# A graph kernel on one core: a DRAM copy in parts of 80 rows, key and digit rows in four buffers each, adding scatters of two groups outstanding

## The chip, the cores and the metric

The kernel runs on one core of a Trainium2 chip. The metric is the device time of one execution in microseconds. The kernel before has a median of 1702.86 us in 3 runs (1702.32 to 1704.51).

## What is computed

There are 50,000 nodes with 256 features each (x), 12,500 edges from `src` to `dst`, with `dst` sorted, and 128 features for every edge. Two layers, cut to what matters:

```
# layer 0, attention over the edges that end in a node
h   = x @ Wn.T + bn
a   = leaky_relu(sum((h[src] + edge_attr @ We.T + be) * attn))
a   = softmax of a over the edges with the same dst
x1  = layernorm(x + relu(segment_sum(h[src] * a, dst)))
# layer 1, mean of neighbours; here the edges are summed by src
agg = segment_sum(x1[dst], src)
out = layernorm(x1 + x1 @ W1.T + b1 + (agg / count) @ W2.T + b2)
```

Most nodes have no edge. So the sum z = x + relu(...) is x for most rows, with a few thousand rows changed.

## The kernel before

Edges are handled in T = 100 tiles of 128, in Q = 25 groups of GT = 4 tiles. The work runs in stages, in the same order on all engines:

1. **Set-up and edge features** (to 80 us). SyncE loads edge features into the four buffers `xin` (lines 349 to 361), twelve loads of eight tiles and two of one; a load waits until VectorE has used the buffer (`s_eau`). VectorE makes a dot product for every tile (`feature_dot`, L783).
2. **Two counting sorts**, by `dst` and then by `src` (80 to 470 us). For each sort VectorE and ScalarE make one-hot rows of all keys' digits (`onehots`, `high_onehots`), TensorE adds them to a histogram, and then, group by group, TensorE adds a tile's one-hots to a table (`count_tile`, L1173), ScalarE copies the table (L648), TensorE looks the tile's keys up in it (L1222), and VectorE reads the found ranks (`found_rank`, `ranks`, `tiles`, L842). Each group needs its keys and its low digits spread over all 128 partitions: SyncE loads both from DRAM (L370, L372), each into two buffers (`lowB`, `kB`), and waits for `s_lbT`, `s_lbA` and `s_kbu` before it overwrites one. ScalarE's part of the digits (`upper_across`, L616) stands one group ahead, in the middle of its table copies (L649).
3. **GpSimd beside them.** It scatters each tile's edges to their sorted places with an indirect transfer (`scatter_order`, L469, at most FLIGHT = 6 outstanding), loads the order, and from the seventh group of the second sort on it gathers the rows x[src] into `X` (L485 to 488). Then it scatters the first 20 tiles of the second sort (`order_src(20)`, L499).
4. **Softmax weights** (to 515 us), from dots of the gathered rows, on VectorE.
5. **First aggregation** (515 to 868 us), `by_dst` on all engines: per group TensorE sums weighted rows with matrices that VectorE makes from the sorted keys (`select`, L987; keys loaded by `load3`, L380), multiplies by Wn, ScalarE cuts at zero into `xin` (L674), and GpSimd adds the four tiles to `z_scratch` with four adding indirect scatters (L508). Rows that aren't the last of their node go to spare rows behind row N. GpSimd waits before a group until the scatters of the group before have landed (L505, L506). Until the first of them `z_scratch` must hold all of x (L500).
6. **Dense stage** (868 to 1455 us) over all 50,000 rows of z, 98 groups, and **second aggregation** (to the end).

**The copy of x to z_scratch** runs from DRAM to DRAM in NCOPY = 100 parts on SyncE's queue (`copy_x`, L344). A part takes every hundredth block of 4 rows of x, which is 125 rows of 4 KB, 500 KB in all. The parts are placed by hand in SyncE's order: 8 before the fifth load of features, one behind each of the first sort's 25 groups, 24 behind the second group of the second sort (two whenever two more groups of one-hots are ready), 11 beside the later groups, and the remaining 32 once the first two loads of sorted keys are issued (L391). The loads of sorted keys of the third group and on come behind those (L392).

Of the kernel before, what the change touches and what calls it, by code (L numbers as in the profile page):

```python
# [5 lines left out]
P = 128  # L6
# [46 lines left out]
def build(nc, x, src, dst, edge_attr, Wn, bn, We, be, attn, W1, b1, W2, b2, out):  # L53
# [14 lines left out]
    NEC = FT // EC  # L68
    NCOPY = 100
    assert N % (NCOPY * GT) == 0  # L70

    z_dram = nc.dram_tensor("z_scratch", [N + 6 * P, D], F32).ap()
    keyrow_dram = [nc.dram_tensor(f"keys_scratch{k}", [T, P], F32).ap() for k in (DST, SRC)]
# [4 lines left out]
    with ExitStack() as ctx:  # L78
        def sb(name, shape, dt=F32):
            return ctx.enter_context(nc.sbuf_tensor(name, shape, dt))  # L80
# [4 lines left out]
        def sems(name, n):  # L85
            return [sem(f"{name}{i}") for i in range(n)]
# [77 lines left out]
        zeros = sel[0]  # L164
        trash_i = sb("trash_i", [P, T], I32)
        trash = sb("trash", [P, T])
# [8 lines left out]
        aggn = sb("aggn", [P, GT, D])  # L175
        lowB = [aggn[:, i, :].bitcast(BF16) for i in range(2)]
        spare16 = aggn[:, 2:4, :].rearrange("p j c -> p (j c)").bitcast(BF16)
# [34 lines left out]
        s_seed = sem("table_seeded")  # L212
        s_kb = sems("key_spread", 2)
        s_kbu = sem("key_spread_used")
        s_lb = sems("low_digit_spread", 2)
        s_lbT = sem("low_onehot_across_ready")
# [104 lines left out]
        def full(ap):  # L321
            return ap[:].rearrange("p j d -> p (j d)")
# [5 lines left out]
        def _(sp):  # L328
# [12 lines left out]
            def part_of(table):  # L341
                return table.rearrange("(r c k) d -> c r (k d)", c=NCOPY, k=GT)

            def copy_x(n):  # L344
                for c in range(copied[0], min(copied[0] + n, NCOPY)):
                    sp.dma_start(part_of(z_dram[0:N])[c], part_of(x)[c]).then_inc(s_copy, 16)  # L346
                copied[0] = min(copied[0] + n, NCOPY)

            for c in range(NEC):
                if c == 4:  # L350
                    copy_x(8)
                wait(sp, s_eau, EC * (c - 3))
                v = edge_attr[0:NEC * EC * P].rearrange("(c t p) d -> p c t d", p=P, t=EC)
                sp.dma_start(full(xin[c % 4]).rearrange("p (t d) -> p t d", d=DE),
                             v[:, c:c + 1].rearrange("p a t d -> p (a t) d")).then_inc(s_ea[c % 4], 16)
# [8 lines left out]
            for k in (DST, SRC):  # L364
                sp.wait_ge(s_keyd[k], 32)
                for q in range(Q):
                    n = k * Q + q
                    wait(sp, s_lbT, n - 1)
                    wait(sp, s_lbA, n - 1)
                    sp.dma_start(lowB[n % 2], spread(lowrow_dram[k], q)).then_inc(s_lb[n % 2], 16)  # L370
                    wait(sp, s_kbu, n - 1)
                    sp.dma_start(full(kB[n % 2]), spread(keyrow_dram[k], q)).then_inc(s_kb[n % 2], 16)  # L372
                    if k == DST or q >= 2 and q % 2:
                        copy_x(1)
                    if k == SRC and q == 1:
                        for i in range(Q // 2):
                            sp.wait_ge(s_onehot, Q + 2 * i + 1)
                            copy_x(2)

# [40 lines left out]
        def _(pool):  # L420
# [5 lines left out]
            g.iota(iota_i, pattern=[[1, LO]], base=0, channel_multiplier=0)  # L426
            g.iota(trash_i[:], pattern=[[0, Q], [P, GT]], base=N + 1, channel_multiplier=1).then_inc(s_iota, 1)
            g.memset(ones[:], 1.0)
# [71 lines left out]
            pool.wait_ge(s_copy, 16 * NCOPY)  # L500
            pool.wait_ge(s_zero, 48)

            for q in range(Q):
                pool.wait_ge(s_relu, 2 * q + 2)
                if q:  # L505
                    pool.wait_ge(s_zsc[(q - 1) % 4], 16 * GT * ((q - 1) // 4 + 1))  # L506
                for j in range(GT):
                    g.indirect_dma_start(out=z_dram, out_offset=column(idx_out[DST], GT * q + j), in_=xin[q % 4][:, j, :],  # L508
                                         in_offset=None, compute_op=ALU.add).then_inc(s_zsc[q % 4], 16)
# [36 lines left out]
        def _(act):  # L546
# [29 lines left out]
            act.wait_ge(s_const, 2)  # L576
            for i in range(3):
                act.dma_start(z_dram[N + 2 * i * P:N + 2 * (i + 1) * P].rearrange("(p r) d -> p (r d)", r=2),
                              full(zeros)).then_inc(s_zero, 16)
# [36 lines left out]
            def upper_across(k, q):  # L616
                n = k * Q + q
                act.wait_ge(s_lb[n % 2], 16 * (n // 2 + 1))
                wait(act, s_look[k], GT * (q - 1))
                if k == SRC and q < 2:  # L620
                    act.wait_ge(s_look[DST], T)
                wait(act, s_lbA, n)
                made = gap(gap_low, lowB[n % 2], -1.0, slot_f[:, 1:2])
                is_zero(onehotT[n % 2][:, 1, :], gap_low, made).then_inc(s_lbA, 1)
# [9 lines left out]
            for k in (DST, SRC):  # L634
                if k == SRC:
                    act.wait_ge(s_add[DST], T)
                for q in range(Q):
                    high_onehots(k, q)
                act.wait_ge(s_hotA, (k + 1) * Q)
                if k == DST:  # L640
                    act.wait_ge(s_bias, 1)
                    act.wait_ge(s_zero, 48)
                upper_across(k, 0)
                act.wait_ge(s_seed, k + 1)
                for i in range(T // 2):
                    wait(act, s_add[k], 2 * i)
                    wait(act, s_look[k], 2 * (i - 1))
                    a.copy(table[i % 2].rearrange("p b c -> p (b c)"), bank[2][:, 0:2 * HC]).then_inc(s_tab, 1)  # L648
                    if i % 2 == 0 and i // 2 + 1 < Q:  # L649
                        upper_across(k, i // 2 + 1)  # L650
                    if k == SRC and i == 2 * ORDER_AT + 5:
                        store_sorted(DST)
# [81 lines left out]
        def _(dve):  # L734
# [19 lines left out]
            v.tensor_copy(iota16[:], iota_i)  # L754
            v.tensor_copy(trash[:], trash_i[:])

# [65 lines left out]
            def low_across(k, q):  # L822

                n = k * Q + q
                dve.wait_ge(s_lb[n % 2], 16 * (n // 2 + 1))
                wait(dve, s_look[k], GT * (q - 1))
                if k == SRC and q < 2:
                    dve.wait_ge(s_look[DST], T)
                ts(onehotT[n % 2][:, 0, :], lowB[n % 2], slot_f[:, 0:1], None, ALU.is_equal).then_inc(s_lbT, 1)

# [11 lines left out]
            def tiles(k, between):  # L842
                low_across(k, 0)
                for q in range(Q):
                    n = k * Q + q
                    for f in between.get(q, ()):
                        f()
                    dve.wait_ge(s_kb[n % 2], 16 * (n // 2 + 1))
                    keys = full(kB[n % 2])
                    for j in range(GT):  # L850
# [541 lines left out]
```

## Time and profile before

| | us |
|---|---|
| median of 3 runs | 1702.86 |
| profiled execution, its own time | 1711.68 |
| its span | 1709.9 |
| TensorE busy | 1276.8 (75%) |
| VectorE busy | 1089.1 (64%) |
| ScalarE busy | 782.5 (46%) |
| GpSimd busy | 747.8 (44%) |
| bytes moved | 260.18 MB, mean 152 GB/s |

All times in the rows are microseconds from the start of the span unless marked otherwise. PE is TensorE, DVE is VectorE, ACT is ScalarE, POOL is GpSimd, and SPq is the queue of SyncE, whose entries are issues of transfers, not the transfers themselves. A bracket behind an instruction gives the idle time of its engine before it and what ended it. The share of a DMA queue is the time that its packets took, as a share of 16 engines' time in the stretch.

### The profile page before, as it was taken

How to read it: one execution, taken by the hardware profiler on the slowest of the kernel's cores; microseconds unless marked ns; L12 is line 12 of the kernel's file. 1: busy time of each engine (PE TensorE's matmuls, PEld its weight loads, DVE VectorE, ACT ScalarE, POOL GpSimd, SP SyncE). 2: the span in 40 equal slices, each digit the busy share in tenths (PEclk: the TensorE clock that was granted, in tenths of full speed). 3: DMA queues.
4: the chain of work that ended last, by engine and by line, in shares of the span. 5: the costliest groups of instructions: out<-in, count | busy, mean ns of one | idle time of the engine just before them, and what ended most of it. 6: DMA issues, size and time to landing. Idle time of an engine off the chain costs nothing.

```text
span 1709.9 us, 26717 instructions
## 1 busy us (share of the span) xinstructions
PE 1276.8 (75%) x7210; PEld 1075.5 (63%) x7210; DVE 1089.1 (64%) x3970; ACT 782.5 (46%) x1768; POOL 747.8 (44%) x731
## 2 busy tenths in 40 slices
PE   4367672276703079988259999999999899999995
PEld 3266652165602068876148888888888688877784
DVE  8655581165691045543048888889898878777762
ACT  6333381143301034443127777777777545444442
POOL 1056630046771046566634443025553336555553
PEclk9689996599856589999669999999999999999998
DMA  4655533367643345555456666678998423232221
GB/s 142 193 147 159 159 118 132 133 168 197 197 168 130 140 88 81 80 80 59 53 136 220 221 220 218 226 238 292 303 296 284 158 70 97 85 91 89 90 85 44
DMA packets 118873, 260.18 MB, mean 152 GB/s; under 512 B 21973, under 2 KB 55340, under 8 KB 118796
## 3 DMA queue, kind: packets, MB, share of 16 engines
q1 hardware_dynamic: 76738, 193.81, 34.5%
q0 software_dynamic: 40128, 64.45, 17.7%
q10 hardware_dynamic: 1930, 1.06, 0.2%
q8 instruction: 28, 0.46, 0.1%
q14 instruction: 49, 0.40, 0.1%
HBM read 182.23 MB, written 129.96 MB: 183 GB/s over the span
## 4 chain that ended last, share of the span: by engine, by line
PE 40%; DMA 22%; SPq 12%; POOL 10%; DVE 8%; issue 6%; ACT 1%; POOLq 0%; ACTq 0%; DVEq 0%
PE bank L1244 25%; DMA aggn<-low_digits_scratch 12%; SPq L346 11%; PE bank L1234 7%; POOL z_scratch L508 5%; DMA z_scratch<-xin,idx_out 5%; DVE X L745 3%; DMA xin<-z_scratch,idx_src 3%; PE bank L1241 3%; POOL out_rows L463 3%; POOL xin L460 2%; PE bank L1289 2%; PE bank L1285 2%; DMA xin<-in_edge_attr 1%; DMA kB<-sorted_scratch 1%
## 5 line engine op out<-in xcount | busy, mean ns | idle before, releaser
L1244 PE MATMUL bank<-w1T,xT 128*128 128x256 f32 x1968 | 492.1, 381 | 0.0
L1244 PEld LDWEIGHTS bank<-w1T,xT 128*128 128x128 f32 x1968 | 344.0, 191 | 66.5 <-issue 0.3
L469 POOL DMA_INDIRECT order_scratch<-pay,rank_i x200 | 194.6, 973 | 257.6 <-DVE rank_i L840 108.1
L562 ACT ACTIVATE yout<-bank,nmr,rstd 128x256 f32<-128x256 f32 x492 | 251.1, 576 | 9.0 <-DVE nmr L748 9.0
L508 POOL DMA_INDIRECT z_scratch<-xin,idx_out x100 | 156.5, 1565 | 188.8 <-DMA z_scratch<-in_x 85.3
L913 DVE BATCH_NORM_STATS2 stats<-xin 128x6 f32<-128x512 f32 x246 | 158.2, 685 | 114.2 <-DMA xin<-z_scratch,idx_src 57.4
L1173 PE MATMUL bank<-X 128*128 128x196 bf16 x800 | 101.6, 265 | 164.0 <-ACT sel L648 140.3
L553 ACT COPY xT<-bank 128x512 f32<-128x512 f32 x346 | 202.9, 588 | 39.9 <-PE bank L1234 32.2
L661 ACT COPY agg<-bank 128x257 f32<-128x257 f32 (+1 forms) x200 | 74.2, 371 | 300.0 <-PE bank L1289 293.6
L913 DVE BATCH_NORM_STATS2 stats<-bank 128x6 f32<-128x512 f32 x246 | 168.4, 693 | 60.3 <-PE bank L1244 59.8
L1173 PEld LDWEIGHTS bank<-X 128*128 128x128 bf16 x800 | 70.5, 104 | 195.3 <-ACT sel L648 155.9
L1285 PE MATMUL bank<-X,sel 128*128 (+2 forms) x400 | 124.6, 395 | 80.6 <-DVE csel L745 80.6
L1222 PE MATMUL bank<-sel,agg 128*128 128x196 f32 x800 | 174.8, 368 | 0.0
L745 DVE TENSOR_SCALAR xin<-xin,stats,rstd 128x256 f32<-128x256 f32 x492 | 172.7, 413 | 1.0
L1234 PE MATMUL bank<-ident,xin 128*128 128x128 f32 x984 | 132.4, 274 | 50.6 <-DVE xin L745 50.6
L557 ACT ACTIVATE std<-stats,eps_c 128x4 f32<-128x4 f32 x271 | 80.9, 299 | 184.9 <-DVE stats L913 176.2
L1241 PE MATMUL bank<-bias,ones 128*128 128x256 bf16 (+1 forms) x592 | 162.1, 274 | 3.2 <-ACT xT L553 2.7
L460 POOL DMA_INDIRECT X<-in_x,idx_src x100 | 98.7, 987 | 150.0 <-DVE idx_out L899 115.1
L463 POOL DMA_INDIRECT out_rows<-yout,idx_out x100 | 99.9, 999 | 144.8 <-DMA xin<-z_scratch,idx_src 74.8
L1234 PEld LDWEIGHTS bank<-ident,xin 128*128 128x128 f32 x984 | 117.7, 142 | 66.0 <-issue 51.2
L460 POOL DMA_INDIRECT X<-z_scratch,idx_dst x100 | 94.8, 948 | 140.8 <-DVE xin L745 110.1
L1222 PEld LDWEIGHTS bank<-sel,agg 128*128 128x128 f32 x800 | 151.5, 217 | 0.2
(187 smaller groups left out, 1915.4 us busy)
## 6 DMA issues: line engine op xcount, KB each, us to landing
z_scratch<-in_x SPq DMA_DIRECT2D x100, 500.0 KB
xin<-z_scratch SPq DMA_DIRECT2D x97, 512.0 KB, 4.1
out_rows<-yout SPq DMA_DIRECT2D x97, 512.0 KB, 3.1
kB<-keys_scratch SPq DMA_DIRECT2D x50, 256.0 KB, 4.7
kB<-sorted_scratch SPq DMA_DIRECT2D x50, 256.0 KB, 3.5
aggn<-low_digits_scratch SPq DMA_DIRECT2D x50, 128.0 KB, 8.6
xin<-in_edge_attr SPq DMA_DIRECT2D x12, 512.0 KB, 6.6
order_scratch<-pay,rank_i POOLq DMA_INDIRECT x200, 5.2
```

What stands on the lines that cost most here:

```text
L346: sp.dma_start(part_of(z_dram[0:N])[c], part_of(x)[c]).then_inc(s_copy, 16)
L460: g.indirect_dma_start(out=dst_ap, out_offset=None, in_=table, in_offset=where).then_inc(s, 16)
L469: g.indirect_dma_start(out=order_dram[k], out_offset=bass.IndirectOffsetOnAxis(ap=rank_i[k][:, t:t + 1], axis=0), in_=pay[:, t, :], in_off ...
L508: g.indirect_dma_start(out=z_dram, out_offset=column(idx_out[DST], GT * q + j), in_=xin[q % 4][:, j, :], in_offset=None, compute_op=ALU.ad ...
L553: a.copy(xT[dst_i][:].rearrange("p a b c -> p (a b c)"), src_bank[:, :]).then_inc(copied, 1)
L562: a.activation(yout[hu][0:rows, j, :], bank_of(j // 2)[0:rows, (j % 2) * D:(j % 2 + 1) * D], ACT.Identity, bias=nmr[0:rows, slot, j:j + 1] ...
L745: return v.tensor_scalar(o, i, s1, s2, o0, o1) if o1 is not None else v.tensor_scalar(o, i, s1, s2, o0)
L913: return v.bn_stats(stats[0:rows, slot, 2 * p:2 * p + 2, :].rearrange("p j s -> p (j s)"), pair.rearrange("p j c -> p c j"))
L1222: ins = mm(bank[3 + t % 4][:, 0:HC], onehotT[n % 2][:, b, j * P:(j + 1) * P], table[i % 2][:, b, :], start=b == 0, stop=b == 1)
L1234: ins = tr(o[:, at:at + n], buf[0:n, 2 * p + jj, c * P:(c + 1) * P], ident[0:n, 0:n])
L1241: mm(to, ones16[:, 0:n], bias16[:, bias, :], start=True, stop=False)
L1244: ins = mm(to, buf[:, jj, c, 0:n], w[:, c, :], start=False, stop=i == len(terms) - 1 and c == 1)
```

## The change

- The copy has 125 parts instead of 100. A part takes every 125th block of 5 rows: 80 rows of 5 KB, 400 KB in all. 12 parts go before the fifth load of features; none stands beside the lookups of either sort; 36 go behind the fourth group of the second sort (three whenever two more groups of one-hots are ready); the remaining 77 go where the last 32 went.
- The spread keys and low digits have four buffers each. They lie in `yout`, which is free until the dense stage; `kB` keeps the sorted keys alone.
- GpSimd waits for the scatters of the group before the last one, so two groups' scatters may be outstanding. The spare rows behind row N are therefore eight blocks in turn instead of four (`trash_i`), and five instead of three transfers clear them. `trash_i` moves into a buffer that is free at that time.

```diff
-    NCOPY = 100
-    assert N % (NCOPY * GT) == 0
-
-    z_dram = nc.dram_tensor("z_scratch", [N + 6 * P, D], F32).ap()
+    NCOPY, CR = 125, 5
+    assert N % (NCOPY * CR * 16) == 0
+
+    z_dram = nc.dram_tensor("z_scratch", [N + 10 * P, D], F32).ap()
...
-        trash_i = sb("trash_i", [P, T], I32)
+        TS = -(-T // (2 * GT)) * 2 * GT
+        trash_i = xT[2][:].rearrange("p a b c -> p (a b c)").bitcast(I32)[:, 0:TS]
...
-        lowB = [aggn[:, i, :].bitcast(BF16) for i in range(2)]
+        lowB = [yout[i][:, 2, :].bitcast(BF16) for i in range(4)]
+        keyB = [yout[i][:, 0:2, :].rearrange("p j c -> p (j c)") for i in range(4)]
...
-                return table.rearrange("(r c k) d -> c r (k d)", c=NCOPY, k=GT)
+                return table.rearrange("(r c k) d -> c r (k d)", c=NCOPY, k=CR)
...
-                    copy_x(8)
+                    copy_x(12)
...
-                    wait(sp, s_lbT, n - 1)
-                    wait(sp, s_lbA, n - 1)
-                    sp.dma_start(lowB[n % 2], spread(lowrow_dram[k], q)).then_inc(s_lb[n % 2], 16)
-                    wait(sp, s_kbu, n - 1)
-                    sp.dma_start(full(kB[n % 2]), spread(keyrow_dram[k], q)).then_inc(s_kb[n % 2], 16)
-                    if k == DST or q >= 2 and q % 2:
-                        copy_x(1)
-                    if k == SRC and q == 1:
+                    wait(sp, s_lbT, n - 3)
+                    wait(sp, s_lbA, n - 3)
+                    sp.dma_start(lowB[n % 4], spread(lowrow_dram[k], q)).then_inc(s_lb[n % 4], 16)
+                    wait(sp, s_kbu, n - 3)
+                    sp.dma_start(keyB[n % 4], spread(keyrow_dram[k], q)).then_inc(s_kb[n % 4], 16)
+                    if k == SRC and q == 3:
                         for i in range(Q // 2):
                             sp.wait_ge(s_onehot, Q + 2 * i + 1)
-                            copy_x(2)
+                            copy_x(3)
...
-            g.iota(trash_i[:], pattern=[[0, Q], [P, GT]], base=N + 1, channel_multiplier=1).then_inc(s_iota, 1)
+            g.iota(trash_i, pattern=[[0, TS // (2 * GT)], [P, 2 * GT]], base=N + 1, channel_multiplier=1).then_inc(s_iota, 1)
...
-                if q:
-                    pool.wait_ge(s_zsc[(q - 1) % 4], 16 * GT * ((q - 1) // 4 + 1))
+                if q >= 2:
+                    pool.wait_ge(s_zsc[(q - 2) % 4], 16 * GT * ((q - 2) // 4 + 1))
...
-            for i in range(3):
+            for i in range(5):
                 act.dma_start(z_dram[N + 2 * i * P:N + 2 * (i + 1) * P].rearrange("(p r) d -> p (r d)", r=2),
                               full(zeros)).then_inc(s_zero, 16)
```

ScalarE and VectorE take the digits and keys from buffer n % 4 instead of n % 2.

## Rows read from the trace of the kernel before

**Rows 1.** The page's section 4, the chain that ended last, its shares by line

```profile
PE bank L1244 25%; DMA aggn<-low_digits_scratch 12%; SPq L346 11%; PE bank L1234 7%; POOL z_scratch L508 5%; DMA z_scratch<-xin,idx_out 5%; DVE X L745 3%; DMA xin<-z_scratch,idx_src 3%; PE bank L1241 3%; POOL out_rows L463 3%; POOL xin L460
```

**Rows 2.** DMA view of 540 to 580 us; queue line: packets, MB, share of 16 engines

```profile
DMA packets 1337, 5.26 MB, mean 132 GB/s; under 512 B 52, under 2 KB 52, under 8 KB 1337
...
q1 hardware_dynamic: 1337, 5.26, 32.0%
```

**Rows 3.** DMA views of the dense stage, 1000 to 1100 and 1200 to 1300 us

```profile
DMA packets 7008, 22.22 MB, mean 222 GB/s; under 512 B 1589, under 2 KB 1603, under 8 KB 7008
...
DMA packets 8861, 29.74 MB, mean 297 GB/s; under 512 B 1605, under 2 KB 1605, under 8 KB 8859
```

**Rows 4.** Timeline of SyncE's queue: start us, us, line, out<-in, count

```profile
22.95 19.53 SPq L346 DMA_DIRECT2D z_scratch<-in_x  x8
...
89.74 0.74 SPq L346 DMA_DIRECT2D z_scratch<-in_x  x1
...
227.39 85.15 SPq L346 DMA_DIRECT2D z_scratch<-in_x  x24
```

**Rows 5.** Timeline of VectorE, the first feature dot behind the copies; idle before in brackets

```profile
62.07 0.29 DVE L748 SCALAR_TENSOR_TENSOR xin<-xin,u_b 128x128 f32<-128x128 f32 x1 [11.30 <-DMA xin<-in_edge_attr]
```

**Rows 6.** Timeline of TensorE, lookups of both sorts; idle before in brackets

```profile
82.15 0.83 PE L1173 MATMUL bank<-X 128*128 128x196 bf16 x4 [0.58 <-ACT sel L648]
...
91.09 0.50 PE L1173 MATMUL bank<-X 128*128 128x196 bf16 x4
...
225.30 0.33 PE L1169 MATMUL bank<-zero 128*128 128x392 bf16 x1
...
265.19 0.83 PE L1173 MATMUL bank<-X 128*128 128x196 bf16 x4 [0.58 <-ACT sel L648]
...
331.65 0.84 PE L1173 MATMUL bank<-X 128*128 128x196 bf16 x4 [58.90 <-ACT sel L648]
...
334.87 0.50 PE L1173 MATMUL bank<-X 128*128 128x196 bf16 x4
...
338.73 0.50 PE L1173 MATMUL bank<-X 128*128 128x196 bf16 x4
```

**Rows 7.** Timelines of VectorE and TensorE, from the last row dot on

```profile
502.79 0.08 DVE L748 DVE_READ_ACCUMULATOR xT<-X,v_b 128x1 f32 x1
...
530.35 1.03 PE L1244 MATMUL bank<-wnT,xT 128*128 128x256 f32 x4
608.61 1.23 PE L1285 MATMUL bank<-X,sel 128*128 128x257 f32 x2 [77.23 <-DVE csel L745]
```

**Rows 8.** Timeline of GpSimd, adding scatters; last line from the chain of waits

```profile
606.03 1.63 POOL L508 DMA_INDIRECT z_scratch<-xin,idx_out  x1 [85.29 <-DMA z_scratch<-in_x]
...
621.00 1.58 POOL L508 DMA_INDIRECT z_scratch<-xin,idx_out  x1 [7.68 <-ACT xin L674]
...
704.10 1.56 POOL L508 DMA_INDIRECT z_scratch<-xin,idx_out  x1 [2.95 <-DMA z_scratch<-xin,idx_out]
...
714.19 1.56 POOL L508 DMA_INDIRECT z_scratch<-xin,idx_out  x1 [2.93 <-DMA z_scratch<-xin,idx_out]
...
864.48 3.79 DMA z_scratch<-xin,idx_out
```

**Rows 9.** Timeline of TensorE, first aggregation, the same step of two neighbouring groups

```profile
703.69 0.60 PE L1285 MATMUL bank<-X,sel 128*128 x2
...
711.93 0.60 PE L1285 MATMUL bank<-X,sel 128*128 x2
```

**Rows 10.** Timeline of GpSimd, order scatters (first line: the page's group: count, busy, mean ns) and gathers

```profile
L469 POOL DMA_INDIRECT order_scratch<-pay,rank_i x200 | 194.6, 973 | 257.6 <-DVE rank_i L840 108.1
...
245.37 0.64 POOL L480 DMA_DIRECT2D ordrow<-order_scratch  x1 [9.15 <-DMA order_scratch<-pay,rank_i]
...
361.11 1.02 POOL L460 DMA_INDIRECT X<-in_x,idx_src  x1 [115.10 <-DVE idx_out L899]
...
493.62 1.08 POOL L460 DMA_INDIRECT X<-in_x,idx_src  x1 [0.30 <-issue]
```

More of the change, by code:

```diff
@@ L212, in build @@
         s_seed = sem("table_seeded")
-        s_kb = sems("key_spread", 2)
+        s_kb = sems("key_spread", 4)
         s_kbu = sem("key_spread_used")
-        s_lb = sems("low_digit_spread", 2)
+        s_lb = sems("low_digit_spread", 4)
         s_lbT = sem("low_onehot_across_ready")
@@ L500, in _ @@
             pool.wait_ge(s_copy, 16 * NCOPY)
-            pool.wait_ge(s_zero, 48)
+            pool.wait_ge(s_zero, 80)
             for q in range(Q):
                 pool.wait_ge(s_relu, 2 * q + 2)
-                if q:
-                    pool.wait_ge(s_zsc[(q - 1) % 4], 16 * GT * ((q - 1) // 4 + 1))
+                if q >= 2:
+                    pool.wait_ge(s_zsc[(q - 2) % 4], 16 * GT * ((q - 2) // 4 + 1))
                 for j in range(GT):
@@ L617, in upper_across @@
                 n = k * Q + q
-                act.wait_ge(s_lb[n % 2], 16 * (n // 2 + 1))
+                act.wait_ge(s_lb[n % 4], 16 * (n // 4 + 1))
                 wait(act, s_look[k], GT * (q - 1))
@@ L622, in upper_across @@
                 wait(act, s_lbA, n)
-                made = gap(gap_low, lowB[n % 2], -1.0, slot_f[:, 1:2])
+                made = gap(gap_low, lowB[n % 4], -1.0, slot_f[:, 1:2])
                 is_zero(onehotT[n % 2][:, 1, :], gap_low, made).then_inc(s_lbA, 1)
@@ L641, in _ @@
                     act.wait_ge(s_bias, 1)
-                    act.wait_ge(s_zero, 48)
+                    act.wait_ge(s_zero, 80)
                 upper_across(k, 0)
@@ L754, in _ @@
             v.tensor_copy(iota16[:], iota_i)
-            v.tensor_copy(trash[:], trash_i[:])
+            v.tensor_copy(trash[:], trash_i[:, 0:T])
             def key_rows(k):
@@ L824, in low_across @@
                 n = k * Q + q
-                dve.wait_ge(s_lb[n % 2], 16 * (n // 2 + 1))
+                dve.wait_ge(s_lb[n % 4], 16 * (n // 4 + 1))
                 wait(dve, s_look[k], GT * (q - 1))
@@ L828, in low_across @@
                     dve.wait_ge(s_look[DST], T)
-                ts(onehotT[n % 2][:, 0, :], lowB[n % 2], slot_f[:, 0:1], None, ALU.is_equal).then_inc(s_lbT, 1)
+                ts(onehotT[n % 2][:, 0, :], lowB[n % 4], slot_f[:, 0:1], None, ALU.is_equal).then_inc(s_lbT, 1)
             def found_rank(k, t):
@@ L847, in tiles @@
                         f()
-                    dve.wait_ge(s_kb[n % 2], 16 * (n // 2 + 1))
-                    keys = full(kB[n % 2])
+                    dve.wait_ge(s_kb[n % 4], 16 * (n // 4 + 1))
+                    keys = keyB[n % 4]
                     for j in range(GT):
```

## The prediction

> **What bounds the kernel now.** I read the chain that ended last first. TensorE's dense products have 25% of it, and the change doesn't touch them. The load of the low digits has 12%, the issue of the copy of x (SPq L346) 11%, the adding scatters and their landings 5% and 5% [rows 1]. These are the stages before 868.3 us, where the last adding scatter lands; all after it, 1709.9 - 868.3 = 841.6 us, I leave as it is. The profiled execution took 1711.68 us with a span of 1709.9; the median of the runs, 1702.86, is 8.8 us lower. I take my difference off the median.
>
> Second, the copy by itself, where nothing else runs: 132 GB/s, with 32.0% of the time of 16 DMA engines used [rows 2]. 32% is 5 of 16 (31%), and a part has 125 rows = 5 x 25: I read it as five engines at 26.3 GB/s each, eleven idle. Loads and stores of 128 rows don't look so: the dense stage moves 222 and 297 GB/s [rows 3].
>
> Third, the stages. The eight early copies keep SyncE's queue from 22.95 to 42.5 us [rows 4], and VectorE then waits 11.30 us for edge features behind them [rows 5]. The first sort's lookups take 82.15 to 225.30 us, 143.15 for 25 groups. In the second sort the burst of 24 copies holds SyncE for 85.15 us [rows 4], the digits of the third group can't be issued until it is over, and TensorE stands for 58.90 us [rows 6]. At the end TensorE stands 77.23 us for sorted keys that are queued behind the copy [rows 7], and the adding scatters wait 85.29 us for it, to 606.03; the last lands at 864.48 + 3.79 = 868.3 [rows 8]. Last, GpSimd runs one group of adding scatters in 714.19 - 704.10 = 10.09 us, of which 2.95 is the wait for the group before to land [rows 8]; TensorE's own group is 711.93 - 703.69 = 8.24 us [rows 9].
>
> **The copy's parts.** 80 rows = 16 x 5, so all 16 engines should share one: 80 x 5,120 bytes = 0.41 MB each; 12 parts go early (4.9 MB), 36 in the burst (14.75 MB), 77 at the end (31.5 MB). The rate is the large unknown. Bounds: below, 132 GB/s (no gain); above, 16 x 26.3 = 420. The nearest row with 16 engines at work on 4 KB rows is the 297 of the dense stage [rows 3], which wasn't yet short of transfers, so I take somewhat more, **330 GB/s**, and keep 297 and 420 for the range. Issuing is no limit: 0.74 us a part [rows 4] is 57 us for 77. The Trainium skill ("DMA: Bandwidth & Descriptors", section on why a DMA increments its semaphore by 16) says that a transfer runs on the largest number of engines up to 16 that divides its slowest dimension on both sides: 5 for 125 rows and 16 for 80. The 32.0% agrees.
>
> **Features.** 4.9 MB is over at 23 + 15 = 38 us, before the fifth load of features is issued. Of the 11.30 us I take back 9.3 (0 to 11.3; a load still has to land). First lookup 82.15 - 9.3 = 72.9.
>
> **First lookups.** Where digits and keys are there, a group takes 338.73 - 334.87 = 3.86 us [rows 6]. With four buffers and no copy beside them, I let all groups run so; the first two took 91.09 - 82.15 = 8.94 instead of 7.72 us, 1.2 more. 25 x 3.86 + 1.2 = 97.7, a gain of 45.4 (bounds: 0, were the loads late anyway, and 45.4). End at 170.6. GpSimd's order scatters do not keep up: 0.97 us and 0.3 between two are 5.1 a group, so they end near 207, wait some 9 us as before [rows 10] and their load lands near 222. That is wanted only in the sixth group of the second sort, near 231: hidden, with 9 us to spare.
>
> **Second lookups.** One-hots and histogram keep their 265.19 - 225.30 = 39.9 us: first lookup at 210.5. ScalarE makes the digits of group q+1 in the middle of group q, and four groups are now loaded ahead of the burst, so the load behind it is wanted at 210.5 + 1.2 + 3 x 3.86 = 223.3, 50.6 us after the burst begins (227.39 - 54.7 = 172.7). At 330 GB/s the burst takes 44.7: no stall (from 291 GB/s down it is one). The 58.90 us go. Lookups end at 210.5 + 97.7 + 2 for the order columns = 310.
>
> **Gathers and softmax.** The 100 gathers took 1.34 us each (361.11 to 495.0, [rows 10]) and start with group 7, now 241: 375, landed 381. From the last dot to the first cut h it is 531.4 - 502.8 = 28.6 us [rows 7]: first scatter possible at 410. The gathers are what is late next: they outlast them by 65 us, and the 20 order scatters behind them on GpSimd (25 us) end at 400, hidden under the softmax.
>
> **The copy's end.** SyncE issues the 77 parts from 310 on. With 48 gathers left (6.3 MB) 37.8 MB go through: 115 us at 330, so 425. The copy is still last, by 15 us. The sorted keys of the third group come behind it, as now.
>
> **Adding scatters.** With two groups outstanding GpSimd needs 4 x (1.56 + 0.30) = 7.5 us a group, less than TensorE's 8.24, which becomes the pace. From the first scatter: 15.0 to the second group (621.00 - 606.03), 23 x 8.24 = 189.5, the last four 7.5, landing 3.8: 215.8 us, against 868.3 - 606.0 = 262.3, a gain of 46.5. TensorE's pace excludes more; below, no row shows two groups in flight, and rival 2 prices no gain. The two more clearing transfers, issued in the first 10 us on ScalarE's queue, cost nothing: their first reader is the lookups' table at 70 us; without that cover they would be some 1 us. The larger iota of spare indices likewise.
>
> **Sum.** 425 + 216 = 640.4 against 868.3: -228 us. 1702.9 - 228 = **1475**.
>
> **Rivals.**
> 1. *All 16 engines, but slower.* Every byte of the copy is both read from and written to DRAM, and no row shows 16 engines doing only that. At the 222 GB/s of the dense stage's first part [rows 3] the burst takes 66 us, a stall of 16, lookups end at 326, the copy at 496: 712, **1546**. The Trainium skill (same page, "Latency and other measured facts") gives 214 GB/s per direction as the full rate of copies between memory tensors; by it 1553. Nothing in this trace bears on it, since five engines reach 132. Chance 0.2.
> 2. *The scatters' pace stays 10.1 us* since two groups in flight only land later: 425 + 262 = 687, **1522**. For it: landings, not issue, are waited for. Against: 4 us of landing overlap 7.5 us of issue. Chance 0.1.
> 3. *Gathers suffer*: the copy used five engines and now uses all. At 2.0 us for each of the last 48, first scatter at 442: **1485**. Against: beside five busy engines they went at 1.38 us [rows 10]. Chance 0.1.
> 4. *Slower: the parts don't spread*, and the copy stays at 131 GB/s. Then taking 25 parts away from the lookups is a loss: features +6 us, burst 113 us with a stall of 62, lookups end at 388, the last 38 MB at 676: 892, +24, **1726**. It decides from about 138 GB/s down. Against: 5 of 16 fits 125 rows too well. This is also how the change would fail to do what it says. Chance 0.04.
>
> **Numbers.** The forecast's own case (297 to 420 GB/s) has 0.56 and reaches from 1454 (copy hidden under the softmax: 410 + 24 x 8.24 + 11.3 = 619) to 1488. Gathers at 1.26 us would take 8 more off: 1446. The range goes from 1446 to 1548, which takes in rivals 1 to 3. 0.2% (3.4 us; the runs lie 2.2 apart) is about what can be told from no change. Faster 0.95, same 0.01, slower 0.04.
>
> **What would show it.** Right: over 300 GB/s and a busy share near 0.9 in the tail of the copy, lookup groups of 3.9 us in both sorts, no stall after the burst, first adding scatter at 410 to 440, then 8.2 us a group. Wrong: a share of 0.32 in the tail (rival 4), a rate near 220 with all engines busy (1), scatters at 10 us (2), gathers at 2 us (3), or lookup groups over 5 us: then something other than digits paces them.

## The result, and the profile after

The changed kernel takes **1483.2 us** in the median of 4 runs (1479.6 to 1485.8), the kernel before 1703.3: a ratio of 0.8706 with a 95% interval of 0.8682 to 0.8730, or 220 us less. The forecast was 1475 (228 less). On another chip the same two gave 1483.2 and 1705.3. One execution of all, of the kernel e4_two_buffers below, took 3416.6 us instead of 1492; no trace of it was kept, its cause is open, and no figure here uses it.

The page of the profiled execution (its own time 1480.68 us): span, busy time, the 40 slices, and the chain that ended last.

```profile
span 1478.9 us, 26741 instructions
...
PE 1243.5 (84%) x7210; PEld 1049.3 (71%) x7210; DVE 1091.8 (74%) x3970; ACT 783.8 (53%) x1768; POOL 749.0 (51%) x731
...
DMA  6754695779975666656666766888974223332221
...
PE bank L1244 31%; PE bank L1234 8%; SPq L348 7%; PE bank L1222 5%; POOL out_rows L463 4%; DMA xin<-z_scratch,idx_src 4%; PE bank L1241 4%; POOL xin L460 4%; PE bank L1289 3%; PE bank L1285 3%; ACT aggn L600 3%; DVE X L745 2%; PE bank L1173 2%; DMA yout<-low_digits_scratch 2%; ACT sel L648 1%
```

The low digits' load had 12% of the chain [rows 1] and has 2%; the adding scatters and their landings, 5% and 5% before, are no longer listed. The issue of the copy is still there, with 7% instead of 11% (its line is now L348): the copy still sets when the adding scatters may begin.

SyncE's queue, the three places of the copy and the load behind the burst (start us, us, line, count):

```profile
24.11 8.69 SPq L348 DMA_DIRECT2D z_scratch<-in_x  x12
...
169.75 34.04 SPq L348 DMA_DIRECT2D z_scratch<-in_x  x36
205.79 0.33 SPq L372 DMA_DIRECT2D yout<-low_digits_scratch  x1
...
314.96 99.67 SPq L348 DMA_DIRECT2D z_scratch<-in_x  x77
```

Against [rows 4]: 24 parts held the queue for 85.15 us, 36 parts with a fifth more bytes in all (14.7 against 12.3 MB) hold it for 34.04.

TensorE, at the ends of its stages (start us, us, line; idle before in brackets):

```profile
70.74 0.83 PE L1173 MATMUL bank<-X 128*128 128x196 bf16 x4 [0.58 <-ACT sel L648]
...
167.69 0.33 PE L1169 MATMUL bank<-zero 128*128 128x392 bf16 x1
...
206.92 0.83 PE L1173 MATMUL bank<-X 128*128 128x196 bf16 x4 [0.58 <-ACT sel L648]
...
231.10 0.83 PE L1173 MATMUL bank<-X 128*128 128x196 bf16 x4 [9.55 <-ACT sel L648]
...
315.37 0.33 PE L1169 MATMUL bank<-zero 128*128 128x392 bf16 x1
385.96 0.46 PE L1264 MATMUL bank<-ident,xdot 128*100 128x128 f32 x1 [70.27 <-DVE xT L748]
...
413.06 1.03 PE L1244 MATMUL bank<-wnT,xT 128*128 128x256 f32 x4
435.76 1.23 PE L1285 MATMUL bank<-X,sel 128*128 128x257 f32 x2 [21.68 <-DVE csel L745]
```

Against [rows 6] and [rows 7]: the first sort's lookups take 97.0 us instead of 143.2, which is 25 groups of 3.86 and a slow start. The stall behind the burst is 9.55 us instead of 58.90, the wait for the keys behind the copy 21.68 instead of 77.23. The wait for the dots of the gathered rows is 70.27 us long; it was half of that before:

```profile
502.93 0.45 PE L1264 MATMUL bank<-ident,xdot 128*100 128x128 f32 x1 [35.19 <-DVE xT L748]
```

The lookups end earlier and the gathers keep GpSimd's own pace, so the last one is issued 64 us after the lookups' end (379.14 against 315.37), and its dots come 70 us after it.

GpSimd's first adding scatters (start us, us, line; idle before in brackets):

```profile
433.18 1.63 POOL L508 DMA_INDIRECT z_scratch<-xin,idx_out  x1 [24.79 <-DMA z_scratch<-in_x]
...
446.79 1.58 POOL L508 DMA_INDIRECT z_scratch<-xin,idx_out  x1 [6.31 <-ACT xin L674]
...
455.03 1.56 POOL L508 DMA_INDIRECT z_scratch<-xin,idx_out  x1 [1.07 <-ACT xin L674]
...
463.28 1.56 POOL L508 DMA_INDIRECT z_scratch<-xin,idx_out  x1 [1.09 <-ACT xin L674]
```

And from the chain of waits, the last one's landing:

```profile
641.36 3.72 DMA z_scratch<-xin,idx_out
```

Against [rows 8]: 463.28 - 455.03 = 8.25 us a group instead of 10.09, and what ends the wait is ScalarE's cut of h at zero, not a landing.

The copy nearly alone, DMA view of 409 to 417 us (a queue's line: packets, MB, time of its packets as a share of 16 engines):

```profile
DMA packets 719, 2.64 MB, mean 330 GB/s; under 512 B 206, under 2 KB 206, under 8 KB 718
...
q1 hardware_dynamic: 615, 2.62, 100.7%
```

The same view of 330 to 380 us, with the gathers beside the copy:

```profile
DMA packets 5005, 18.61 MB, mean 372 GB/s; under 512 B 1134, under 2 KB 1134, under 8 KB 5004
...
q1 hardware_dynamic: 3219, 13.74, 73.0%
```

And the busy shares of 414 to 434 us in 40 slices, in which the last parts land, with GB/s below them:

```profile
DMA  9999999999998999998999876432210000000000
GB/s 338 328 389 420 348 338 317 348 348 379 358 338 287 352 358 328 328 348 320 352 305 289 274 283 180 180 133 102 92 66 31 20 31 20 31 31 20 25 25 16
```

Against [rows 2]: 330 GB/s with all 16 engines busy, instead of 132 with 32.0%. That is 20.6 GB/s an engine against 26.3. The rate isn't even: 404 to 416 us gives 314 GB/s with 224 packets of the order scatters beside the copy, 416 to 424 us 341 with none. In the last rows the share begins to fall near 425 us, and from 429.5 to 433.2 us some 25 GB/s are left, with 6.2% of the 16 engines' time, which is one engine. The engines don't finish together, and the copy is done only when the last one is.

### The profile page after: what moved, and what is told of

It reads as the page before. It is cut to its first block, busy times and chain, and to the rows that moved or that the text cites. A ratio compares the mean times of both kernels' runs of the same rounds, so it can differ in the third digit from the quotient of the medians.

```text
span 1478.9 us, 26741 instructions
## 1 busy us (share of the span) xinstructions
PE 1243.5 (84%) x7210; PEld 1049.3 (71%) x7210; DVE 1091.8 (74%) x3970; ACT 783.8 (53%) x1768; POOL 749.0 (51%) x731
## 4 chain that ended last, share of the span: by engine, by line
PE 55%; POOL 9%; DMA 8%; issue 7%; ACT 7%; SPq 7%; DVE 6%; ACTq 0%; POOLq 0%; DVEq 0%
PE bank L1244 31%; PE bank L1234 8%; SPq L348 7%; PE bank L1222 5%; POOL out_rows L463 4%; DMA xin<-z_scratch,idx_src 4%; PE bank L1241 4%; POOL xin L460 4%; PE bank L1289 3%; PE bank L1285 3%; ACT aggn L600 3%; DVE X L745 2%; PE bank L1173 2%; DMA yout<-low_digits_scratch 2%; ACT sel L648 1%
## 5 line engine op out<-in xcount | busy, mean ns | idle before, releaser
L1222 PE MATMUL bank<-sel,agg 128*128 128x196 f32 x800 | 155.6, 338 | 0.1
L1173 PE MATMUL bank<-X 128*128 128x196 bf16 x800 | 94.4, 252 | 48.8 <-ACT sel L648 23.6
L1289 PE MATMUL bank<-agg,csel 128*128 128x257 f32 (+1 forms) x396 | 123.1, 393 | 12.2 <-ACT agg L661 12.2
L1222 PEld LDWEIGHTS bank<-sel,agg 128*128 128x128 f32 x800 | 133.0, 194 | 0.5 <-DVE bank L748 0.3
```

Of the source, the lines that this page charges most:

```text
L1222: ins = mm(bank[3 + t % 4][:, 0:HC], onehotT[n % 2][:, b, j * P:(j + 1) * P], table[i % 2][:, b, :], start=b == 0, stop=b == 1)
L1289: ins = mm(o, csel[u % 2][:, j, :], before, start=False, stop=True)
```

## Experiments

Where the expectation names the kernel before or the changed kernel, the difference is against these two. Between chips the medians of the kernel before were 1703.3 to 1705.6.

**How many engines carry a part.** The changed kernel, the same bytes in the same places, but parts of 125 rows (e2_rows125, the diff) and of 100 rows (e3_rows100, with `NCOPY, CR = 100, 5`).

```diff
-    NCOPY, CR = 125, 5
-    assert N % (NCOPY * CR * 16) == 0
+    NCOPY, CR = 100, 4
+    assert N % (NCOPY * CR) == 0
...
-                    copy_x(12)
+                    copy_x(10)
...
-                            copy_x(3)
+                            copy_x(3 if i < 5 else 2)
```

> The changed kernel, but with the copy in 100 parts of 125 rows of 4 KB as before (10 parts early, 29 in the burst, 61 at the end: the same bytes in the same places). Theory: the number of rows sets how many engines carry a part, 5 for 125, so the copy runs alone at 131 GB/s with a busy share near 0.32. Then the features start some 19 us later, the burst of 14.85 MB takes 113 us and the lookups stand for 60 to 70 us behind it, the end of the copy is near 640, and the time is 1690 to 1730 us, about that of the kernel before. Rival: bytes per row or the missing copies beside the lookups made the copy fast, not its row count; then it runs at over 250 GB/s here too and the time stays within 1475 to 1510.

Measured: **1713.2 us**, ratio 1.0036 [1.0009, 1.0064], so slower than before by 0.1 to 0.6%. The copy alone, 500 to 540 us:

```profile
DMA packets 1337, 5.27 MB, mean 132 GB/s; under 512 B 51, under 2 KB 51, under 8 KB 1337
...
q1 hardware_dynamic: 1337, 5.27, 32.0%
```

The same 132 GB/s and 32.0% as before. The last 61 parts end at 659 us, and what the other parts of the change give is lost again. That is the fourth rival, nearly at its price (1726). Not all of it is the five engines: e10_buffers_five_engines below has them too, but its parts in their old places, and takes 1611.1 us.

> The changed kernel, but with the copy in 100 parts of 100 rows of 5 KB (10 early, 29 in the burst, 61 at the end, the same bytes in the same places). With 80 rows all engines are busy, but each moves only 19.6 GB/s where the copy is alone, against 26.3 with five. Theory: that is a limit that all share, not the engines' own; 100 rows run on ten engines, a share of 0.62, at 25 to 26 GB/s each, 240 to 263 together, and the end of the copy is 5 to 20 us later: 1485 to 1505 us. Rival: rows of 5 KB cost each engine more, and ten give 196 GB/s; then the last 31 MB take some 175 us and the time is 1530 to 1560. Second rival: the row count doesn't matter in this way and all 16 engines stay busy: 1483.

Measured: **1517.6 us**, ratio 0.8883 [0.8824, 0.8942]. The copy alone, 430 to 448 us:

```profile
DMA packets 1022, 4.76 MB, mean 265 GB/s; under 512 B 92, under 2 KB 92, under 8 KB 1022
...
q1 hardware_dynamic: 1022, 4.76, 63.6%
```

63.6% is ten engines of 16 (62.5%), at 26.2 GB/s each with rows of 5 KB. So the row's size doesn't slow an engine: with the same rows of 5 KB ten engines give 26.2 each and sixteen 20.6, which points to something that they share. Both rivals fall. The time is 12 us above the theory's range all the same, and the copy's end came 34 us late (467.4 against 433.2), not 5 to 20. 10 us of this are there before the last parts start, mostly since the stall behind the burst is 18.46 us instead of 9.55. Then the copy is slower, by most beside the gathers, with 198 GB/s (340 to 370 us) where sixteen engines gave it 275:

```profile
q1 hardware_dynamic: 1274, 5.93, 48.1%
```

I had not counted that a part of the gathers' rows passes through the copy's ten engines and takes time there (48.1% instead of 63.6%).

**The buffers.** The changed kernel with two buffers each.

```diff
-                    wait(sp, s_lbT, n - 3)
-                    wait(sp, s_lbA, n - 3)
-                    sp.dma_start(lowB[n % 4], spread(lowrow_dram[k], q)).then_inc(s_lb[n % 4], 16)
-                    wait(sp, s_kbu, n - 3)
-                    sp.dma_start(keyB[n % 4], spread(keyrow_dram[k], q)).then_inc(s_kb[n % 4], 16)
-                    if k == SRC and q == 3:
+                    wait(sp, s_lbT, n - 1)
+                    wait(sp, s_lbA, n - 1)
+                    sp.dma_start(lowB[n % 2], spread(lowrow_dram[k], q)).then_inc(s_lb[n % 2], 16)
+                    wait(sp, s_kbu, n - 1)
+                    sp.dma_start(keyB[n % 2], spread(keyrow_dram[k], q)).then_inc(s_kb[n % 2], 16)
+                    if k == SRC and q == 1:
```

ScalarE and VectorE take the digits and keys from buffer n % 2 again.

> The changed kernel with two buffers each for keys and low digits, as before, and the burst behind the second group of the second sort, since only two groups can be loaded ahead. Theory A: the two buffers cost time even with no copy beside the lookups, because each load is issued only when the digits two groups before are made; a lookup group takes 4.4 to 5.1 us instead of 3.86, which with 10 us more of stall behind the burst gives 1510 to 1550 us. Theory B: with the copy away a load lands in 3 to 4 us and two buffers are enough; groups stay at 3.9 us and only the stall behind the burst grows: 1488 to 1500.

Measured: **1492.7 us**, ratio 0.8741 [0.8666, 0.8815]. Theory B. TensorE's end of the first sort and its stall in the second:

```profile
167.60 0.33 PE L1169 MATMUL bank<-zero 128*128 128x392 bf16 x1
...
229.52 0.84 PE L1173 MATMUL bank<-X 128*128 128x196 bf16 x4 [15.95 <-ACT sel L648]
```

The first sort ends at 167.60 as with four buffers (167.69). The stall behind the burst comes two groups earlier and is 15.95 us long, 6.4 more, and by as much the adding scatters begin later (439.6 against 433.2). That is what the traces show of the 9.5 us; the rest lies behind the last landing (838.4 us instead of 833.8), within what other runs show there. With no copy beside the lookups, four buffers shorten no lookup group.

**The adding scatters.** The changed kernel with one group outstanding, and the kernel before with two.

```diff
-                if q >= 2:
-                    pool.wait_ge(s_zsc[(q - 2) % 4], 16 * GT * ((q - 2) // 4 + 1))
+                if q:
+                    pool.wait_ge(s_zsc[(q - 1) % 4], 16 * GT * ((q - 1) // 4 + 1))
```

> The changed kernel with the wait for the adding scatters of the group just before, so that one group is outstanding. Theory: GpSimd goes back to 10.1 us a group against TensorE's 8.24, which costs 24 x 1.85 = 44 us: 1525 to 1532 us. Rival: the longer group came from the order in which buffers of xin came free, which is gone since the aggregation starts otherwise, and it costs less than 20 us: under 1503.

Measured: **1534.1 us**, ratio 0.8977 [0.8915, 0.9039], 51 us more than the changed kernel (expected 42 to 49). A later group's first scatter waits for landings again:

```profile
456.56 1.56 POOL L508 DMA_INDIRECT z_scratch<-xin,idx_out  x1 [2.99 <-DMA z_scratch<-xin,idx_out]
...
467.21 1.56 POOL L508 DMA_INDIRECT z_scratch<-xin,idx_out  x1 [3.50 <-DMA z_scratch<-xin,idx_out]
```

The other way round, the kernel before with this wait, the spare rows, the index pattern and the five clearing transfers of the change, and nothing else of it:

> The kernel before with only the last part of the change: adding scatters of two groups may be outstanding (and the spare rows and clearing transfers that go with it). Theory: the pace of 8.24 instead of 10.1 us a group is worth the same wherever the stage begins, 24 x 1.85 = 44 to 51 us as taken out of the changed kernel: 1650 to 1662 us. Rival: it is worth less here, over 1675.

Measured: **1659.3 us**, ratio 0.9737 [0.9709, 0.9765], 46 us less. The copy ends as late as before, and the groups after it run at TensorE's pace (634.98 - 626.73 = 8.25 us):

```profile
626.73 1.60 POOL L509 DMA_INDIRECT z_scratch<-xin,idx_out  x1 [0.97 <-ACT xin L675]
...
634.98 1.56 POOL L509 DMA_INDIRECT z_scratch<-xin,idx_out  x1 [1.05 <-ACT xin L675]
```

**The spread alone.** The kernel before with parts of 80 rows, two buffers and one group of scatters.

```diff
-    NCOPY = 100
-    assert N % (NCOPY * GT) == 0
+    NCOPY, CR = 125, 5
+    assert N % (NCOPY * CR * 16) == 0
...
-                return table.rearrange("(r c k) d -> c r (k d)", c=NCOPY, k=GT)
+                return table.rearrange("(r c k) d -> c r (k d)", c=NCOPY, k=CR)
...
-                    copy_x(8)
+                    copy_x(10)
...
-                        copy_x(1)
+                        copy_x(2 if q % 4 == 3 else 1)
...
-                            copy_x(2)
+                            copy_x(2 + i % 2)
```

> The kernel before with nothing changed but the copy's parts: 125 parts of 80 rows of 5 KB, the same bytes in the same places (10 parts early, 1 beside each lookup group and a second beside every fourth, 30 in the burst, the rest at the end), two buffers, one group of adding scatters. Theory: sixteen engines are the larger share of the 220 us; features 9 us earlier, lookup groups near 4.5 us since a load waits 1.5 us instead of 4 behind a part (30 us and 20 us), the stall behind the burst 20 instead of 59 us, the copy's end hidden under gathers and softmax, and 10.1 us a group after it: 1540 to 1590 us. Rival: the placement of the parts matters more than their rate, and the loads of digits stay late beside copies: 1600 to 1650.

Measured: **1529.0 us**, ratio 0.8982 [0.8951, 0.9014]: 176 us less from the row count alone, more than I expected. The waits for low digits, before and here (engine, line, releaser: us, times, longest), and the first adding scatter here:

```profile
ACT aggn L600 <- DMA aggn<-low_digits_scratch: 193.1, 36, 59.9
...
ACT aggn L600 <- DMA aggn<-low_digits_scratch: 67.9, 20, 12.8
...
434.32 1.63 POOL L508 DMA_INDIRECT z_scratch<-xin,idx_out  x1 [10.43 <-ACT xin L674]
```

The digits are still late beside the parts (67.9 us of waits instead of 193.1), the first sort takes 119.6 us (71.46 to 191.04), and yet the first adding scatter comes at 434 us, as in the changed kernel (433): there it waits for the copy, here only for h. What e1 lacks against the changed kernel is the pace of the scatters, 51 us by e5, and it is only 46 us slower, since its second group follows at once (444.58) where the changed kernel waits for h until 446.79.

**Five engines with the other parts of the change.** The changed kernel with parts of 125 rows, placed as before but for the burst, which stays behind the fourth group. Except for this place and the four buffers it is e9_two_groups_only.

```diff
-    NCOPY, CR = 125, 5
-    assert N % (NCOPY * CR * 16) == 0
+    NCOPY, CR = 100, 4
+    assert N % (NCOPY * CR) == 0
...
-                    copy_x(12)
+                    copy_x(8)
...
+                    if k == DST or q >= 2 and q % 2:
+                        copy_x(1)
                     if k == SRC and q == 3:
...
-                            copy_x(3)
+                            copy_x(2)
```

> The changed kernel, but with the copy in 100 parts of 125 rows and placed as before (8 early, 1 beside each lookup group, 24 in the burst, now behind the fourth group of the second sort, the rest at the end); four buffers and two groups of scatters stay. Theory: four buffers hide a part's 3.9 us at most partly, since one part a group of 3.86 us keeps the five engines full; lookup groups of 4.5 to 5 us in the first sort, a stall of 40 to 50 us behind the burst, the copy's end near 525: 1560 to 1600 us. Rival: the loads stay as late as before, groups of 5.7 us: 1620 to 1650.

Measured: **1611.1 us**, ratio 0.9453 [0.9425, 0.9481], between the two expectations. DMA issues of 100 to 170 us, with the median time to landing:

```profile
yout<-keys_scratch SPq DMA_DIRECT2D x14, 256.0 KB, 14.6
yout<-low_digits_scratch SPq DMA_DIRECT2D x13, 128.0 KB, 15.9
```

A load takes 15.9 us to land where it took 8.7 before: with four buffers it is issued earlier, behind parts that fill five engines, and a lookup group still takes 5.4 us, near the 5.7 of before. By this alone one would say that depth doesn't help where the engines are full. The time says otherwise. On the same chip e9_two_groups_only took 1659.3 us, so the four buffers, with the place of the burst that they allow, are worth 48 us here. ScalarE's waits for low digits, in e9_two_groups_only and here:

```profile
ACT aggn L601 <- DMA aggn<-low_digits_scratch: 178.8, 33, 59.2
...
ACT aggn L602 <- DMA yout<-low_digits_scratch: 143.2, 31, 54.3
```

The first sort ends 6 us earlier (216.84 against 222.87). Most of the gain lies behind the burst, where a part stands beside every second group only: there 21.5 groups take 4.1 us each, where 23.5 took 5.8, and the lookups end at 414.2 instead of 464.8.

**Parts beside the first sort's lookups.** The changed kernel with parts put back beside them, and a burst of 24. The diff is e6_one_beside's: one part a group. e7_two_beside has `copy_x(2)` there, e11_best_spread `copy_x(2 if q % 4 == 3 else 1)`, and e8_one_beside_two_buffers is e6_one_beside with the two buffers of e4_two_buffers.

```diff
+                    if k == DST:
+                        copy_x(1)
                     if k == SRC and q == 3:
...
-                            copy_x(3)
+                            copy_x(2)
```

> The changed kernel with one part of 80 rows beside each lookup group of the first sort and 24 in the burst, so that 64 parts are left for the end instead of 77. Theory: beside the first sort the engines stand half idle; 0.8 MB a group in 3.86 us is 207 GB/s and hides; the shorter burst ends in time for the fifth group's digits (10 us less stall) and the copy ends before the softmax does, so the first adding scatter comes at 400 to 410 us instead of 433 and has no second stall behind it: 1445 to 1460 us. Rival: parts beside the lookups make the digits late again, whatever the buffers; lookup groups go to 4.5 us or more and the gain is lost: 1475 to 1495.

Measured: **1454.9 us**, ratio 0.8545 [0.8517, 0.8573]. The first sort's lookups take as long as without copies (it ends at 168.27), there is no stall behind the burst, and the scatters begin at 405:

```profile
405.15 1.63 POOL L510 DMA_INDIRECT z_scratch<-xin,idx_out  x1 [9.16 <-DMA z_scratch<-in_x]
```

> As e6_one_beside with two parts beside each lookup group of the first sort, 39 left for the end. Theory: 1.2 MB a group in 3.86 us is 314 GB/s, at what the engines gave for the copy alone (314 to 330), so loads queue behind parts, and GpSimd's order scatters with them; lookup groups of 4 to 4.5 us in the first sort, 4 to 16 us lost there, nothing to gain at the end since the copy is hidden already: 1450 to 1475, at least as long as e6_one_beside. Rival: four buffers hide that too: the same time as e6_one_beside.

Measured: **1455.0 us**, ratio 0.8535 [0.8501, 0.8568], as e6_one_beside. Theory and rival both allow this time; the trace has the theory's loss: the lookups lose 5.6 us (the first sort ends at 173.87). The start of the scatters is no longer the copy's to set, and there is no second wait behind it, which pays the loss back. DMA view of 80 to 160 us:

```profile
DMA packets 10926, 23.69 MB, mean 296 GB/s; under 512 B 2863, under 2 KB 5344, under 8 KB 10916
...
q1 hardware_dynamic: 9295, 23.49, 97.4%
```

> As e6_one_beside, but with two buffers each for keys and digits, and the burst of 24 behind the second group of the second sort. Two buffers cost nothing in the lookups where no copy ran beside them. Theory: with a part of 1.3 us ahead of every load they are too few; groups of the first sort take 4.2 to 5 us, 10 to 28 us more, and behind the burst the digits of the third group come 5 to 10 us late: 1465 to 1495 us. Rival: a part spread over sixteen engines delays a load so little that two buffers suffice: within 10 us of e6_one_beside.

Measured: **1467.6 us**, ratio 0.8613 [0.8585, 0.8640], 12.7 us more than e6_one_beside. The first sort ends at 179.84 instead of 168.27, and the waits for digits sum to 30.6 us (12 times) instead of 10.0 (once). Here four buffers shorten the first sort.

> As e6_one_beside, with a second part beside every fourth group of the first sort, so that 58 parts are left for the end instead of 64. In e6_one_beside the first adding scatter waits 9.2 us for the copy and TensorE 3.7 us for the keys behind it. Theory: the copy then ends under the softmax, first scatter from the chain of gathers at 403 to 405 us and no second stall, 2 to 6 us off: 1449 to 1454 us. Rival: as in e7_two_beside, the lookups pay back what the end gains: 1455.

Measured: **1448.7 us**, ratio 0.8499 [0.8476, 0.8522], the fastest of all, 34.5 us below the changed kernel on the same chip. The first scatter waits for h alone, and the second group follows at once:

```profile
404.26 1.63 POOL L510 DMA_INDIRECT z_scratch<-xin,idx_out  x1 [7.44 <-ACT xin L676]
...
411.96 1.62 POOL L510 DMA_INDIRECT z_scratch<-xin,idx_out  x1 [0.43 <-ACT xin L676]
```

The changed kernel as it is, beside e11_best_spread:

> The changed kernel itself on the same chip as the three others. Expected 1480 to 1486 us as before; if it lies apart from that, comparisons between chips need that much room.

Measured: **1483.2 us**, ratio 0.8699 [0.8676, 0.8721].

## Why the prediction held, and where not

| step | predicted | measured |
|---|---|---|
| copy alone | 330 GB/s | 314 to 341 |
| first lookup | 72.9 | 70.7 |
| first sort's lookups end | 170.6 | 167.7 |
| second sort's first lookup | 210.5 | 206.9 |
| stall behind the burst | 0 | 9.6 |
| lookups end | 310 | 315.4 |
| dots done | 381 | 386.0 |
| first scatter possible | 410 | 414.1 |
| copy landed | 425 | 433.2 |
| last scatter landed | 640.4 | 645.1 |
| difference of medians | -228 | -220 |

**The row count and the engines.** Right, and shown by three points: 125, 100 and 80 rows give shares of 32.0%, 63.6% and 100%. The Trainium skill's rule ("DMA: Bandwidth & Descriptors", on why a DMA increments its semaphore by 16) gives 5, 10 and 16 engines; the traces agree. The rate of 330 GB/s was my choice between 297 and 420, not worked out from any row; that the copy came so near it is luck.

The same page's figure of 214 GB/s per direction for copies between memory tensors ("Latency and other measured facts") is not what this copy shows, 330 GB/s; it was taken from copies of 128 rows of 16 KiB with padded row pitch, which no run here has. (By that figure my own sum gives 1555 us, not the 1553 that I wrote.)

**The burst, the term that was off.** I took the burst's 14.75 MB at 330 GB/s and ended it 6 us before the fifth group's digits were wanted. ScalarE stood ready for these digits at 219.0. Their load was issued in time, at 205.79, and landed 23.4 us later, at 229.2, behind what SyncE had queued. From the burst's begin that is 59.4 us, 248 GB/s for the copy's bytes; the term was mis-sized by 15 us. Two things were left out. In 172 to 205 us the engines were as busy as ever and moved 288 GB/s, with 615 packets of the order scatters among them. The end of the copy, too, was slower with such packets beside it (314 against 341), but no run leaves them out, so whether they are the cause isn't shown. And a load behind a burst lands when the slowest engine has worked off its share: the rows of 414 to 434 us show that for the copy's end, for the burst it is inferred. With 24 parts in the burst, as in e6_one_beside, there is no stall.

**The tail.** 37.8 MB at 330 GB/s were to take 115 us and took 118 (314.96 to 433.2). The mean was right, as a mean of three rates that I had not told apart: 372 GB/s with the gathers, 314 to 341 after them, and an end of 8 us in which the engines run dry one after another. The lookups' late end moved the whole by 5 us.

**Buffers.** The 45 us of the first lookups came, but not from the four buffers, to which I put them together with the missing copies: e4 has two and the same lookups. In the changed kernel they are worth 9.5 us, of which the stall behind the burst shows 6.4. They pay where parts run beside the lookups: 12.7 us on all engines (e8 against e6), 48 on five (e10 against e9).

**Scatters.** 8.25 us a group, predicted 8.24; 211.9 us from the first scatter to the last landing, predicted 215.8. Worth 46 us in the kernel before and 51 in the changed one; the second rival falls.

**Gathers.** 1.32 us each (248.33 to 380.1): the third rival falls. They went at 1.29 us before the last 77 parts and at 1.36 beside them, where five engines at work gave 1.38.

**The stretch after the last landing** was taken as unchanged, 841.6 us. It is 833.8 in the trace after, and 832.5 to 839.4 in those of the twelve experiments. So the one profiled execution of the kernel before was probably some us long there, which would be a part of the 8.8 us by which it lay over its median; no second trace of it tells. Between the two traces the last landing moved by 223.2 us (868.3 to 645.1), where the forecast had 227.9, and the stretch behind it by 7.8: 231.0 in all, against 220 between the medians.

**What the parts are worth.** In a row on one chip: two groups of scatters 46 us (1705.3 to 1659.3), then four buffers with the burst behind the fourth group 48 (to 1611.1), then 16 engines with the new places of the parts 128 (to 1483.2). Alone on the kernel before: spread 176, two groups 46. Out of the changed kernel: spread 230, two groups 51, buffers 9.5. The ways differ since the waits cover for one another, and since the new places suit fast parts only: with five engines, four buffers and two groups, they cost 102 us (e2 against e10). One part of the change costs time even so, the empty engines beside the first sort: putting parts back there gains 28 to 34.5 us.

## What to carry to other kernels

A busy share of DMA that stands at a round fraction of 16 while nothing else runs is a transfer that doesn't use all engines: look at the outer dimension of both its sides, and make it a multiple of 16 before moving transfers about. When a background transfer becomes fast, put it back where engines are idle, in pieces of which one and the loads beside it fit into a step at the measured rate, and size the ring of buffers for a load that lands behind one piece. Judge such a ring by the waits of the engines that read it, not by a load's time from issue to landing, and by more than one stage. A load that is wanted soon after a burst must be reckoned to land when the slowest engine is done with the burst, not at the burst's bytes over the mean rate.

## What the hardware showed that I had not expected

- Five and ten engines copy from DRAM to DRAM at 26.3 and 26.2 GB/s each, sixteen at 20.6 each (132, 265, 330 GB/s; by stretch 314 to 341 with sixteen). With gathers into SBUF beside it the sum is 372 GB/s, of which the copy has 275. What the limit is wasn't tried.
- The copy's last parts: 18.9 us from the issue of a load behind them (414.67) to its landing, in the last 8 us of which engine after engine falls idle; in the last 3.7 us one is left (6.2% of 16, 25 GB/s).
- A longer time to landing isn't a loss by itself: behind five full engines a load of low digits takes 15.9 us to land with four buffers and 8.6 with two (e10, e9), since it is issued earlier, and yet the waits for digits fall from 178.8 to 143.2 us and the kernel is 48 us shorter.
